# Attention loops of a transformer kernel written out, and the products of its cross phases in strips of 32 output rows

## The reference

```
a0: x += proj(attend(q(adaLN(x)), kv(adaLN(ctx))))          # cross, 1601 keys
s1: x += g * proj(attend(qkv(mod(LN(x)))))                  # self, 256 keys
c1: x += proj(attend(q(LN(x)), kv(ctx)))                    # cross, 1601 keys
m1: x += g * mlp(mod(LN(x)))
s2, c2, m2: the same again, with kv(LN(ctx)) in c2
l3: one-head cross attention, three experts and a gate
```

## Time and profile before

| | us |
|---|---|
| median of 3 runs | 6330.64 |
| the profiled execution | 6341.07 |
| span of its trace | 6338.2 |
| TensorE busy (PE) | 5710.4 |
| ScalarE busy | 4218.7 |
| VectorE busy | 4121.8 |
| GpSimd busy | 985.0 |

### The profile page before, as it was taken

The page is one execution under the profiler, slowest core; times in us unless marked ns, Lnnn a source line. Parts: engine busy times, 40 slices in busy tenths (PEclk is TensorE's granted clock), DMA queues, the critical chain, the costliest instruction groups (busy, mean ns, idle before and its releaser), DMA issues.

```text
span 6338.2 us, 195036 instructions
## 1 busy us (share of the span) xinstructions
PE 5710.4 (90%) x73336; PEld 3364.7 (53%) x73336; DVE 4121.8 (65%) x6523; ACT 4218.7 (67%) x8158; POOL 985.0 (16%) x1660
## 2 busy tenths in 40 slices
PE   5999999999877899999999877789999999999998
PEld 3555555555444455555555444445555555545665
DVE  5777777777555677777777455467777777754443
ACT  3777777777666677777777556567777777763333
POOL 3121121121111111111111011212212211200000
PEclk9999999999999999999999989899999999999999
DMA  2222222212111222222222011122222222220110
GB/s 86 83 68 61 83 63 66 83 58 69 46 56 60 84 72 72 68 85 73 72 68 78 2 59 58 56 77 71 60 81 71 64 77 73 63 63 21 55 57 26
DMA packets 229802, 410.32 MB, mean 65 GB/s; under 512 B 23904, under 2 KB 131472, under 8 KB 228624
## 3 DMA queue, kind: packets, MB, share of 16 engines
q1 hardware_dynamic: 229136, 400.04, 21.1%
HBM read 316.81 MB, written 83.14 MB: 63 GB/s over the span
## 4 chain that ended last, share of the span: by engine, by line
PE 73%; ACT 8%; DVE 7%; issue 7%; DMA 2%; SPq 1%; POOL 1%; ACTq 0%; DVEq 0%; POOLq 0%
PE bank L1086 27%; PE bank L1194 17%; PE pair L1086 16%; ACT P L1330 3%; DVE MX L1494 3%; DMA QP<-scr_q 2%; PE pair L1181 2%; PE bank L699 1%; PE bank L690 1%; PE pair L626 1%; ACT QP L1341 1%; DVE ST L1451 1%; PE pair L463 1%; PE pair L722 1%; PE bank L469 1%
## 5 line engine op out<-in xcount | busy, mean ns | idle before, releaser
L1330 ACT ACTIVATE P<-bank 128x512 f32<-128x512 f32 (+1 forms) x5504 | 3090.1, 598 | 1187.8 <-PE bank L1086 1137.0
L1494 DVE TENSOR_REDUCE MX<-pair 128x2 f32<-128x802 f32 x3072 | 2919.6, 987 | 1110.7 <-PE pair L1086 1092.5
L1086 PE MATMUL bank<-QP,KP 128*32 128x256 bf16 (+2 forms) x25600 | 2136.1, 274 | 191.3 <-ACT P L1330 140.1
L1086 PE MATMUL pair<-KP,QP 96*32 96x401 bf16 (+2 forms) x16198 | 1770.9, 334 | 136.5 <-DMA QP<-scr_q 95.9
L1194 PE MATMUL bank<-P,VA 128*25 128x256 f32 (+1 forms) x22016 | 1748.0, 387 | 11.4 <-ACT RS L1336 9.5
L1086 PEld LDWEIGHTS bank<-QP,KP 128*32 128x32 bf16 (+2 forms) x25600 | 1023.7, 98 | 1308.2 <-ACT P L1330 639.4
L1086 PEld LDWEIGHTS pair<-KP,QP 96*32 96x32 bf16 (+1 forms) x16198 | 717.6, 97 | 279.2 <-DVE MX L1494 102.1
L1194 PEld LDWEIGHTS bank<-P,VA 128*25 128x25 f32 (+1 forms) x22016 | 516.3, 103 | 457.3 <-issue 278.6
L1498 DVE TENSOR_REDUCE MX<-pair 128x4 f32<-128x1024 f32 x256 | 311.0, 1222 | 322.2 <-PE pair L1086 321.7
L1619 POOL COPY VA<-VN 128x416 f32<-128x416 f32 (+1 forms) x320 | 140.2, 439 | 2415.5 <-ACT VN L1321 1219.7
L1341 ACT CAST QP<-pair 2x512 bf16<-2x512 f32 x640 | 339.4, 576 | 136.2 <-PE pair L1181 130.5
(11 more groups left out here) (242 smaller groups left out, 4296.4 us busy)
## 6 DMA issues: line engine op xcount, KB each, us to landing
KP<-scr_k SPq DMA_DIRECT2D x768, 225.1 KB
QP<-scr_q SPq DMA_DIRECT2D x960, 48.0 KB
CN<-ctx_n SPq DMA_DIRECT2D x40, 768.0 KB
scr_k<-KSF SPq DMA_DIRECT2D x48, 600.8 KB, 3.2
scr_k<-KSF SPq DMA_DIRECT2D x48, 600.0 KB, 3.3
CT<-ctx_t SPq DMA_DIRECT2D x24, 800.5 KB, 4.5
KP<-scr_ks SPq DMA_DIRECT2D x128, 144.0 KB
scr_q<-QS SPq DMA_DIRECT2D x80, 192.0 KB, 2.1
```

The source lines that it names most:

```text
L1086: last = nc.tensor.matmul(out[c:c + m, :], lhsT[:, c:c + m], rhs, start=start, stop=stop)
L1330: nc.scalar.activation(P[v % 2][0:kt, half * 2 * N:(half + 1) * 2 * N], SC[half][0:kt, :], ACT.Exp, scale=SCALE).then_inc(sem("probs_full" ...
L1494: nc.vector.tensor_reduce(MX[:, r, c:c + 2], MP[j % 2][:, :].rearrange("p (t k) -> p t k", t=2)[:, :, 0:SPANS[0][1]], AX.X, ALU.max).then_ ...
```

## The change

The loops of the attention phases become Python loops on all five engines, so that elements 1 to 14 are straight code with constant counts and addresses. In the cross phases every slot has `first` = `then` = 32, and the `among` pieces of odd slots are no longer moved behind. `mean` goes through `strips_of`. An `among` piece whose name is in `SHORT` is made in strips of 32; all other pieces stay 128 wide.

```
+SHORT = ["mean", "var", "q", "k0", "k1", "k2", "k3", "y"]
...
-                    with loop(sp, 1, B - 1) as i:
+                    for i in range(1, B - 1):
                         prepare(ph.el["middle"](i))
...
-                    last = nc.tensor.matmul(MISC[:, 0:N], w("mean"), xcols(b), start=True, stop=True)
+                    last = strips_of(cols, MISC[:, 0:N], w("mean"), xcols(b))
...
-                            first, then = (32, 128) if (g * ph.nt + t) % 2 else (128, 32)
-                            if first == 32:
-                                among, behind = [], among + behind
+                            first, then = 32, 32
                         scores(ph, b, g, t, 0, first)
                         for j in js[:third]:
                             maximum(*ahead, j, first)
                         for piece_ in among:
-                            piece(el, *piece_)
+                            piece(el, *piece_, first if piece_[1] in SHORT else 128)
```

More of the change, by code:

```diff
@@ L1250, in _ @@
                     element(ph.el["first"])
-                    with loop(pe, 1, B - 1) as i:
+                    for i in range(1, B - 1):
                         element(ph.el["middle"](i))
@@ L1376, in _ @@
                     element(ph.el["first"])
-                    with loop(act, 1, B - 1) as i:
+                    for i in range(1, B - 1):
                         element(ph.el["middle"](i))
@@ L1548, in _ @@
                     element(ph.el["first"])
-                    with loop(dve, 1, B - 1) as i:
+                    for i in range(1, B - 1):
                         element(ph.el["middle"](i))
@@ L1641, in _ @@
                     element(ph.el["first"])
-                    with loop(pool, 1, B - 1) as i:
+                    for i in range(1, B - 1):
                         element(ph.el["middle"](i))
```

## The result

The changed kernel takes 6272.40 us (median of 4 runs, 6269.78 to 6276.06) where the kernel before takes 6332.63 us on the same chip: a ratio of 0.9904, with a 95% interval from 0.9892 to 0.9916. That is 60 us off, and the forecast was 143. Direction right, size wrong by more than half, and the time lies outside the range. The profiled executions have spans of 6338.2 and 6274.1 us, 64.1 apart.

A forecast was written before the change was run, and what follows sets the result against it. It took TensorE's own sequence to bound the cross phases and chains of short steps the self phases. 138 us from strips plus 5 from loops, 143 off the profiled 6341.07, gave 6198, so a median of 6188; 8-in-10 range 6120 to 6255.

The forecast's parts named there:

- the price of a change of width: TensorE, cross phases: switching between whole products and strips costs about 0.1 us each way, 0.2 for the two.
- the rule on column tiling and fast weight loads: TensorE's strip loads: by the skill's rule they would cost more and lose part of 1.1 us per group; trace disagreed.
- the loops are worth little by themselves: All engines: writing out the loops gains 5 us: 7 from first turns, 8 in self elements, minus 10 for constant waits.
- The lower bound for the loops, −45: Loops' worst case: no first-turn gain in the cross phases and 0.12 us lost in every group.
- the sum over the head groups: Cross phases: 2.7 us gained per element of a0 and c2, 3.2 of c1, over 16 elements each: 138 us.
- moving the odd slots' pieces ... starts them about 0.9 us earlier: Odd slots, a0 and c2: k0's 0.31 us wait for t1's copy should go, gaining 0.3 us per element.
- 25% of free time covers: ScalarE, moved odd-slot pieces: scores 1 come up to 0.85 us later; its free time absorbs the late start.
- 11 changes lie ahead of tile 11: 11 x 0.1: Each head group of 13 tiles: width changes removed before tile 11 gain 1.1 us, 4.4 us per element.
- the whole pieces at 0.2 each: Pieces left wide between strips cost 0.2 us each: 1.4 per element of a0 and c2, 1.0 of c1.
- margin of 0.02: Head groups 1 to 3: TensorE's new period 2.81 us stays above VectorE's 2.79, so the whole gain passes.
- There I take off 0.4: Head group 0, where VectorE has more work: gain reduced by 0.4 us in a0 and c2, 0.2 in c1.
- VectorE takes over: Rival: VectorE's period holds wherever maxima run, only about 0.05 of 0.2 us saved there; 6273 us, chance 0.11.

The follow-up runs named there:

- e7: Changed kernel with VectorE's reductions in the cross phases reading only the first half of each span's columns: 6107.45 us, ratio 0.9650.
- e1: Kernel before, its widths as they were, with only the loops over the elements written out: 6320.89 us, ratio 0.9982.
- e2: Strips alone: changed kernel with the loops over the elements kept and mean left whole: 6316.28 us, ratio 0.9972.
- e3: Changed kernel with the pieces of odd slots back behind the value products, all still in strips: 6275.45 us, ratio 0.9911.
- e9: Changed kernel with ScalarE's copy of t1 and t2 moved from behind both exponentials to between them: 6252.67 us, ratio 0.9869.
- e8: Changed kernel with one more ScalarE copy of 0.6 us, read by nobody, for each k piece: 6353.41 us, ratio 1.0038.
- e4: Changed kernel with d, e and v0 to v3 in strips too, t0 to t3 still whole: 6240.43 us, ratio 0.9859.
- e5: Changed kernel with e4's strips, and of the odd slots' pieces only t1 and t2 back behind the value products: 6207.64 us, ratio 0.9797.
- e12: e5 plus an unread TensorE product in the wait ending head group 0, and eight statistics, not nine, ahead of the last maximum: 6176.38 us, ratio 0.9754.
- e6: Changed kernel with five of VectorE's 13 statistics, not nine, ahead of head group 0's last maximum: 6269.26 us, ratio 0.9907.

## Why the prediction was wrong, and where it was right

**Right: the price of a change of width** where nothing else is near: 3.01 to 2.84 for two tiles (0.17 for two changes; e7, with VectorE out of the way, 2.78). The cost that the forecast drew from the rule on column tiling and fast weight loads (the Trainium skill, "TensorEngine Tiling (Array Packing)", Gotcha 2) doesn't show after the change either: the 38400 loads of the scores in strips last 96 ns in the mean, 97 before, and whole ones before 100. **Right: the loops are worth little by themselves** (5 forecast, 12 in e1), with the first turn's stop (2.5 us in `s1`) and the 0.1 per group both as they were read from the rows. (The lower bound for the loops, −45, doesn't come out of its own terms: 5 for the self phases' first turns, −14 and −20 make −29.) But the one number for the pair of edits assumed that they add. They don't: in e2 about 14 us are lost to stops inside the loop of `a0` and 11 to stops at the edges of the loops.

**Wrong: the sum over the head groups.** By the quartiles the 48 elements of the cross phases gained 62 us (16 x (0.73 + 2.34 + 0.81)), with 138 forecast. By group, forecast as in the sum's steps and measured, in `a0`, `c1`, `c2`:

```
         forecast         measured            short by, x 16
group 0  0.3  0.5  0.3    1.06   1.25   1.06     -36
group 1  0.8  1.1  0.8   -0.61   0.66  -0.53      51
group 2  0.9  0.9  0.9   -0.03   0.12  -0.03      42
group 3  0.7  0.7  0.7    0.31   0.31   0.31      19
```

*Group 1: the step "moving the odd slots' pieces ... starts them about 0.9 us earlier", +0.3.* This is the largest failure. It looked at when the piece starts and not at who empties its bank: ScalarE's copy comes behind an exponential that now waits for scores behind the piece. It is worth 1.0 and 0.8 us by e3, 0.83 and 0.62 by e9. (That `c1`, which has no t pieces, is short by 0.4 as well fits k0 and k1, as in group 2.) The sentence that ScalarE's "25% of free time covers" the late start used an average over the phase, which the text had warned of itself a page earlier.

*Group 2: the step "11 changes lie ahead of tile 11: 11 x 0.1".* Only the slots without k pieces are TensorE's. From the start of the group to behind k3, and in group 1 around k0 and k1, ScalarE sets the pace (e8). The value products in order of time say it by slot (group 2 of `c1`, lower quartiles over the elements 2 to 13): from the last slot of group 1 to slot 4 of group 2 they are 10.80 us apart before and 10.79 after, from slot 4 to slot 9 7.27 and 6.96, and from slot 9 to slot 11, where v0 stands alone between strips, 3.31 and 3.51. I had seen this for k1 and t2 in slot 23 and had made an exception of it for two changes; it is the rule wherever a k piece is copied out.

*Group 3, and the whole pieces at 0.2 each.* These were sized about right: v2 and v3 measured 0.30 to 0.57 for the two (forecast 0.4), v0 with v1 0.33 (0.2 for v0, nothing for v1), d and e 0.60 in `c1` (0.4). It is the gross of 1.1 that isn't there even with all of them in strips: e4's group 3 is 0.61 to 0.88 below the kernel before. The "margin of 0.02" that let the whole gain through was too thin: e7 finds 0.38 more in this group, 0.23 to 0.35 in group 1 and 0.19 in group 2, which VectorE holds.

*Group 0: the step "There I take off 0.4".* The place was right and the size was not. The group gained 1.06 (0.27 of it by the loops, e1) and has 2.9 more to give if VectorE is eased (e7). The rival *VectorE takes over* gave 6273, the measured time, but by luck: it let 0.05 of the 0.2 per pair of tiles through, and 0.17 came through. Where VectorE has taken over, and by how much, is group 0 of two phases.

**Missing: the clock.** In the forecast the clock was a risk for the self phases only. In the changed kernel 15.7 of the 23.0 us of excess in the cross phases are groups 1 whose clock fell. The kernel before has 12.7 us of excess, and its granted clock is 1.00 in all of those groups; more than half of its excess lies in groups 0, nearly all with a longer wait for an exponential at their start. Net the cross phases lost 10 us more than before.

In sum, 138 − 76 (the four groups) − 10 (the excess) = 52 us; the remaining 12 of the 64 us lie in first turns, phase ends and the self phases. What stays open: what decides whether the clock falls behind a wait of 1.76 us; why the instructions come late at one place of `a0`'s body in e2, and how much longer a body must be for it; and the excess in group 3 of e4, e5 and e12. In e5 it is 25 us over 18 elements: 8.7 in five with a stop for instructions, 12.2 in eight with a wait of 0.7 to 1.7 us for the load of the packed queries (`QP<-scr_q`), and the rest without a stop over 0.45 us; in three of the 18 the clock fell. No run takes any of these away.

## What to carry to other kernels

When an engine is relieved, go through the stretch slot by slot and ask in each who is next and by how much; a free quarter on average hides slots with nothing to spare. A piece of work in a shared buffer costs its place in the queue of the engine that empties it, not only in the one that fills it. Compare groups and not totals: e3 and e6 moved the time by nothing and each moved single groups by over a microsecond, and their good halves made the best version.

## What the hardware showed that I had not expected

In the changed kernel TensorE's clock fell to its lower level behind 8 of 28 equal waits of 1.76 us, at a cost of 1.3 to 3.0 us each, and behind none of 28 waits of 1.65 us in the kernel before. A product that nobody needs, 1.1 us long, kept it up in all 28 and made the kernel 15 us faster. Strips that run without a gap in the changed kernel's straight code stop once per turn for 0.6 to 2.0 us in the loop of `a0`, 2.4 to 2.7 us behind a packet of the instruction queue, and with six more pieces in strips such stops come in straight code too. And two edits worth 12 and 17 us alone were worth 60 together.
